# A message-passing kernel: the first edge layer and the middle node stage in one block

## The reference

```
h = maximum(layernorm(x), 0)
x = x + L0(h, edge_index, edge_weight, edge_weight_n2)   # signed cosine propagation
h = maximum(layernorm(x), 0)
x = x + L1(h, edge_index)                                # MLP messages, MLP update

L0: Wh = h @ W + b;  Wr, Wc = Wh[row], Wh[col]
    sim = dot(Wr, Wc) / max(|Wr| |Wc|, 1e-8)
    base = adj_v * softplus(deg_coeff[0] * deg_v + deg_coeff[1]) * (row != col)
    prop_pos = segment_sum(base * relu(sim) * Wc, row);  prop_neg likewise of -relu(-sim)
    result = scale * (coeff[0] * prop_pos + coeff[1] * prop_neg + coeff[2] * Wh)
L1: msgs = mlp(concat(x[dst], x[src]));  agg = segment_sum(msgs, dst)
    result = mlp(concat(x, agg))
```

## Time and profile before

| | us |
|---|---|
| median of 3 runs | 2410.95 |
| profiled execution, its own time | 2418.68 |
| its span, first to last instruction | 2416.6 |
| first edge layer, first SP issue to last scatter issue | 205.16 to 1508.13 |
| middle node stage, first SP load to last DVE instruction | 1518.05 to 1641.07 |
| second edge layer, first SP issue to last DVE instruction | 1646.96 to 2190.36 |
| node stage 2, first SP load | 2193.05 |

### The profile page before, as it was taken

How to read it: one execution, slowest core, us unless ns; L and a number is a source line. 1 busy time by engine, 2 the same in 40 slices (tenths; PEclk the granted TensorE clock), 3 DMA queues, 4 the chain that set the end, 5 groups by cost and what they waited for, 6 DMA issues and landing times. The chain is left out here.

```text
span 2416.6 us, 57279 instructions
## 1 busy us (share of the span) xinstructions
PE 1562.8 (65%) x16004; PEld 1340.6 (55%) x16004; DVE 1553.3 (64%) x5636; ACT 864.0 (36%) x3093; POOL 1695.9 (70%) x1413
## 2 busy tenths in 40 slices
PE   4886755455555555555555550005999999997998
PEld 2555645455554545545455550004999999994554
DVE  5995655555555454554545552794999999995554
ACT  3773322222222222222222221462333333334665
POOL 2775888888888888888888886746777777761322
PEclk9996555555555555555555555556999999999999
DMA  3775544444444444444444432565555454534664
GB/s 100 251 247 172 114 82 80 77 83 75 84 79 78 84 74 85 80 77 83 75 86 73 84 47 18 170 221 146 128 124 126 124 126 124 126 81 119 188 188 145
DMA packets 342563, 273.11 MB, mean 113 GB/s; under 512 B 144834, under 2 KB 273514, under 8 KB 342484
## 3 DMA queue, kind: packets, MB, share of 16 engines
q1 hardware_dynamic: 259028, 233.22, 33.2%
q0 software_dynamic: 81536, 38.61, 15.0%
q10 hardware_dynamic: 1920, 0.37, 0.1%
HBM read 206.69 MB, written 65.34 MB: 113 GB/s over the span
## 5 line engine op out<-in xcount | busy, mean ns | idle before, releaser
L1117 POOL DMA_INDIRECT x<-e_sums,e_to x392 | 623.4, 1590 | 126.4 <-issue 118.6
L1352 PE MATMUL bank<-e_parts,e_same 128*128 128x64 bf16 x2940 | 172.8, 240 | 586.7 <-DVE e_parts L1211 586.7
L1304 PE MATMUL bank<-e_window,e_onehot 128*128 128x64 f32 x2352 | 525.0, 422 | 16.8 <-DMA e_window<-wh 16.8
L1304 PEld LDWEIGHTS bank<-e_window,e_onehot 128*128 128x128 f32 x2352 | 511.7, 332 | 16.9 <-DVE e_onehot L1143 16.9
L1102 POOL DMA_INDIRECT e_ends<-wh,e_ids x392 | 425.2, 1085 | 132.8 <-issue 102.1
L1352 PEld LDWEIGHTS bank<-e_parts,e_same 128*128 128x128 bf16 x2940 | 159.4, 129 | 602.8 <-issue 602.8
L829 POOL DMA_INDIRECT e_near_source<-h,e_near_ids x392 | 394.8, 1007 | 129.8 <-issue 117.4
L1250 ACT ACTIVATE e_sq<-e_ends 128x64 f32<-128x64 f32 x784 | 188.6, 241 | 686.0 <-DMA e_ends<-wh,e_ids 685.9
L1175 DVE SCALAR_TENSOR_TENSOR e_prod<-e_ends 128x64 f32<-128x64 f32 x392 | 65.7, 223 | 370.8 <-DMA e_ends<-wh,e_ids 370.8
L939 PE MATMUL bank<-e_near_to_edge,e_near_window 128*64 128x128 f32 x2352 | 153.4, 281 | 171.2 <-DMA e_near_window<-h 171.2
L939 PEld LDWEIGHTS bank<-e_near_to_edge,e_near_window 128*64 128x64 f32 x2352 | 130.0, 139 | 177.6 <-DVE e_near_to_edge L850 171.6
(11 more groups left out here) (150 smaller groups left out, 2860.9 us busy)
## 6 DMA issues: line engine op xcount, KB each, us to landing
e_window<-wh SPq DMA_DIRECT2D x392, 96.0 KB
e_near_window<-h SPq DMA_DIRECT2D x392, 96.0 KB
e_owners<-ends SPq DMA_DIRECT2D x98, 256.0 KB, 2.9
n_x<-x SPq DMA_DIRECT2D x98, 256.0 KB, 3.0
n_x<-in_x_dram SPq DMA_DIRECT2D x49, 256.0 KB, 2.8
wh<-n_wh SPq DMA_DIRECT2D x49, 256.0 KB, 2.0
x<-n_x SPq DMA_DIRECT2D x49, 256.0 KB, 2.3
e_rel<-rel SPq DMA_DIRECT2D x98, 128.0 KB, 3.2
```

The costliest lines, as they stand in the source:

```text
L1117: pool.indirect_dma_start(out=added_tab, out_offset=bass.IndirectOffsetOnAxis(ap=t.to[s][:, j:j + 1], axis=0), in_=t.sums[s][:, j, :], in_ ...
L1304: last = nc.tensor.matmul(bank[s % 2][:, j * D:(j + 1) * D], onehot, window, start=w == 0, stop=w == WK - 1)
L1352: last = nc.tensor.matmul(bank[6 + s % 2][:, i * D:(i + 1) * D], t.same[s][:, same_block(j, i), :], t.parts[s][:, part, j, :], start=j == ...
```

## The change

The block of the first edge layer and that of the middle node stage become one. The edge buffers are allocated and given back before the block, then `agg_sb` and the node stage's buffers are allocated, on the same addresses as before. In the one block each engine runs its edge program and then, with no barrier between, its node program. SP clears the first set of semaphores where it did, and then waits itself for the four `added` semaphores before it loads `x1`. The helper functions that were local to `edge_programs` become functions of the module (`both_ways`, `edge_sync`, `edge_gpsimd`, `edge_vectors`, `edge_scalars`, `edge_tensors`), with what they do unchanged.

```diff
@@ build
-        edge_phase(nc, c, tabs, layer=0, done=first)
-        first.give_back()
+        with ExitStack() as own:
+            edges = EdgeBuffers(c, Slots(nc, c, own, "e0"), 0)
         c["agg"] = sb("agg_sb", [P, NB * D])
         c["sems"] = Semaphores(nc)
-        node_phase1(nc, c, tabs, done=second)
+        edge_and_node_phase(nc, c, tabs, edges, first, second)
+        first.give_back()
         c["sems"] = Semaphores(nc)
-        edge_phase(nc, c, tabs, layer=1)
+        edge_phase(nc, c, tabs)
@@
-def node_phase1(nc, c, tabs, done):
+def edge_and_node_phase(nc, c, tabs, edges, before, done):
@@ block.sync
         def _(sp):
+            edge_sync(nc, sp, c, tabs, edges, edges, 0)
+            before.clear(sp)
+            for s in range(ESLOTS):
+                sp.wait_ge(edges.added[s], 16 * G * -(-(GROUPS - s) // ESLOTS))
+
             def store(s, k):
@@ block.vector
         def _(dve):
+            edge_vectors(nc, dve, c, edges, edges, 0)
+
@@ block.gpsimd
         def _(pool):
+            edge_gpsimd(nc, pool, c, tabs, edges, edges, 0)
+
@@ block.scalar
         def _(act):
+            edge_scalars(nc, act, c, edges, edges, 0)
+
@@ new
+        @block.tensor
+        def _(pe):
+            edge_tensors(nc, pe, c, edges, edges, 0)
+
```

More of the change, by code:

```diff
@@ L718, in _, with edge_phase @@
                                    (-3, normed)])
-def edge_phase(nc, c, tabs, layer, done=None):
+        @block.tensor
+        def _(pe):
+            edge_tensors(nc, pe, c, edges, edges, 0)
+def edge_phase(nc, c, tabs):
     with ExitStack() as ctx:
[L723 to L729, removed]
-        with nc.Block() as block:
-            edge_programs(nc, block, c, tabs, near, far, layer, done)
@@ L734, in edge_programs @@
[L734 to L776, removed]
@@ new lines, in edge_phase, with _ @@
+        with ExitStack() as own:
+            near = NearBuffers(c, Slots(nc, c, own, "e1"))
+        far = EdgeBuffers(c, Slots(nc, c, ctx, "e1"), 1)
+        with nc.Block() as block:
+            @block.sync
+            def _(sp):
+                edge_sync(nc, sp, c, tabs, near, far, 1)
+            @block.gpsimd
+            def _(pool):
+                edge_gpsimd(nc, pool, c, tabs, near, far, 1)
+            @block.vector
+            def _(dve):
+                edge_vectors(nc, dve, c, near, far, 1)
+            @block.scalar
+            def _(act):
+                edge_scalars(nc, act, c, near, far, 1)
+            @block.tensor
+            def _(pe):
+                edge_tensors(nc, pe, c, near, far, 1)
@@ new lines, in both_ways, with edge_sync, apart @@
+def both_ways(c, eng, close, apart):
+    is_near = eng.value_load(c["near"][0:1, 0:1], min_val=0, max_val=1)
+    with eng.If(is_near > 0):
+        close()
+    with eng.Else():
+        apart()
+def edge_sync(nc, sp, c, tabs, near, far, layer):
+    def apart():
+        edge_loads(nc, sp, c, tabs, far, layer, False)
+        if layer == 1:
+            for s in range(ESLOTS):
+                sp.wait_ge(far.added[s], 16 * G * -(-(GROUPS - s) // ESLOTS))
+            sp.dma_start(c["agg"][:].rearrange("p (b d) -> p b d", d=D),
+                         tabs["agg"][0:NB * P, :].rearrange("(b p) d -> p b d", p=P)).then_inc(far.numbers_in[0], 16)
+            sp.wait_ge(far.numbers_in[0], 16 * (1 + -(-GROUPS // ESLOTS)))
+    both_ways(c, sp, lambda: edge_loads(nc, sp, c, tabs, near, layer, True) if layer == 0 else near_sync(nc, sp, c, tabs, near),
+              apart)
@@ new lines, in edge_gpsimd, with edge_vectors @@
+def edge_gpsimd(nc, pool, c, tabs, near, far, layer):
+    both_ways(c, pool, lambda: edge_pool(nc, pool, c, tabs, near, layer, True) if layer == 0 else near_pool(nc, pool, c, tabs, near),
+              lambda: edge_pool(nc, pool, c, tabs, far, layer, False))
+def edge_vectors(nc, dve, c, near, far, layer):
+    both_ways(c, dve, lambda: edge_vector(nc, dve, c, near, layer, True) if layer == 0 else near_vector(nc, dve, c, near),
+              lambda: edge_vector(nc, dve, c, far, layer, False))
@@ L779, with edge_scalars, edge_tensors @@
+def edge_scalars(nc, act, c, near, far, layer):
+    both_ways(c, act, lambda: edge_scalar(nc, act, c, near, layer, True) if layer == 0 else near_scalar(nc, act, c, near),
+              lambda: edge_scalar(nc, act, c, far, layer, False))
+def edge_tensors(nc, pe, c, near, far, layer):
+    both_ways(c, pe, lambda: edge_tensor(nc, pe, c, near, layer, True) if layer == 0 else near_tensor(nc, pe, c, near),
+              lambda: edge_tensor(nc, pe, c, far, layer, False))
 class NearBuffers:
```

## The result

The changed kernel takes 2406.82 us (median of 18 runs) against 2415.58 us of the kernel before on the same chips (18 runs); ratio 0.9965, 95% interval 0.9955 to 0.9976. That is 0.35% less, where 0.31% was forecast. The forecast of 2403.4 us was made from three runs of before whose median, 2410.95, lies low among the eighteen (2408.41 to 2421.45), so the ratio is the better measure of the change. Taken by itself, 2406.82 us lies nearer to the first rival's 2406.2 than to the forecast; the profile has to decide between the two.

A forecast was written before the change was run, and what follows sets the result against it. The prediction saw POOL's scatters bounding before the seam, DVE behind it, and an all-idle hole between. Loads 7.65 us earlier less 0.15 for POOL gave 7.5 us, from 2410.95 to 2403.4 us; range 2402.3 to 2407.5.

The forecast's parts named there:

- the first rival: Middle seam: POOL's own passage remains the gate and the handshake is cheap; gain 4.5 to 5.5 us, time 2406.2; chance 0.17.
- What bounds it and the stock: Seam from first edge layer to middle node stage: all engines idle, 7.7 us to take; DVE's stage behind moves whole.
- The barrier goes: At the seam SP waits only for the scatters' landing; first load at 1510.4, gain there at most 8.4 us.
- The loads meet no other traffic: First `x1` loads start 7.65 us earlier, at 1510.4 instead of 1518.05, with no other traffic that they did not meet before.
- POOL: After its landing wait POOL jumps to the node code, ready at 1514.1 where 1513.95 is needed; 0.15 us charged.
- The number: Sum at the seam: 7.65 - 0.15 = 7.5 us gain, median 2410.95 to 2403.4 us, 0.31% less.
- the 1.4 us that the prediction took for a barrier: Seam from node stage 0 to first edge layer: last store's landing at 203.76 to SP's first DMA at 205.16.
- The 3.6 us that the prediction left unexplained: Rest of the hole after second code packet and 1.4 us of barrier, from 1514.4; perhaps collecting of reports behind scatters.
- The second rival: Middle seam: SP's node code isn't at hand when its wait ends; first load at 1515.1, gain 2.9, time 2408.0; chance 0.06.
- The third: Second edge layer's loop: shifted code crosses a page, each of 20 rounds fetches again, 68 us, time 2471; slower, chance 0.03.

The follow-up runs named there:

- told before the jump: Changed kernel, but SP waits for a semaphore POOL raises behind its own landing wait, before its jump; last scatter's issue end to first `x1` load 1.78 us.
- told after: Changed kernel, but SP waits for a semaphore POOL raises as its first node-stage instruction, behind its jump; last scatter's issue end to first load 4.25 us.
- drained and told: Changed kernel, but SP waits for a semaphore raised by a POOL drain behind its jump; scatter's issue end to first load 9.72 us; timed later, 2415.34 us, ratio 1.0002.

## Why the prediction was right

*What bounds it and the stock.* Right: the hole was on every path, and the node stage moved as a whole: from DVE's first total to its last instruction 120.45 us became 120.38.

*The barrier goes.* The load was put 2.27 us behind the scatter's issue (1510.4) and comes after 1.52. The landing was read from POOL's next scatter, and, as the bound allowed, at least 0.6 us of that was POOL's own way from wait to issue. Gain at the load 8.40 us, the upper bound, not 7.65.

*The loads meet no other traffic.* Wrong by 0.73 us: this step took the load's 2.57 us over unchanged. They came to 3.30, because POOL's jump now falls into the same moment and its code packet (at 1504.3 us in the profile after, 0.9 behind the load's issue) is in the load's way. With the packet out of the way, by code left out or by POOL's wait moved, it is 2.65 and 2.64 again.

*POOL.* Charged 0.15 us, measured nothing. The lateness was bounded by DVE's passage at the last seam, which holds a barrier; POOL's own jump is 2.47 us.

*The number.* The prediction put the gain at the first load 0.75 us too low, overlooked a loss of 0.73 on the load's way to DVE, and charged 0.15 for POOL that did not come: 7.5 + 0.75 - 0.73 + 0.15 = 7.67. The mechanism was right, but that the sum comes this close is luck: two errors of the same size with opposite signs.

*The first rival* was half right: the meeting of five engines is cheap (0.2 to 0.3 us) and the hole was POOL's passage. But that passage did not stay in the load's way. Of the 1.4 us that the prediction took for a barrier at the seam from node stage 0, 0.9 were not the barrier's: without the far way the same seam takes 2.80 us from the last store's issue, not 3.70. The 9.92 us are

| | us | from |
|---|---|---|
| last scatter's landing seen by SP | 1.5 | the changed kernel |
| handover from POOL | 0.3 | told before the jump, less the changed kernel |
| jump with its fetch | 2.5 | told after less told before |
| first drain after indirect DMAs | 5.5 | drained and told, less told after |
| the barrier over that handover | 0.2 | the kernel before, less drained and told |

The change takes POOL's jump and its drain off the path. By the reading above it does not take the drain out of the program, since the block still ends in a barrier, now behind the node stage. There it costs nothing that shows. POOL's last centring ends at 1623.52, SP issues stores until 1629.43, and SP begins the second edge layer 5.88 us after DVE's end, against 5.89 before the change. The 3.6 us that the prediction left unexplained, and laid to the collecting of reports, fall in the 5.5 us of the drain.

The Trainium skill ("Runtime: NRT & Kernel Launch", The launch sequence) puts the meeting of the five engines in the runtime's own barrier at about 355 ns. The 0.34 us of one more barrier agree. The Trainium skill also says (same page, Instruction fetch mechanics) that a taken branch to a page that isn't held forces a fetch before execution goes on. The one packet in the 2.47 us of the jump agrees.

*The second rival* fails: SP was ready. *The third* too: from 1790 to 2120 us in the profile after, the second edge layer's loop, only the data queues move.

```profile
q1 hardware_dynamic: 45290, 33.00, 35.9%
q0 software_dynamic: 8044, 8.26, 14.9%
```

## What to carry to other kernels

Where the last engine to arrive at a barrier is the one that has issued indirect DMAs, look for its drain, 5.5 us here, and not at the meeting, 0.2 to 0.3 us. Let another engine wait for the landing and put the stages in one block, or at least let the issuing engine go to the barrier without waiting while another waits (4.2 of the 8.4 us for an edit of three lines). Put POOL's wait for its scatters behind its jump, not in front, so that its code comes while the last ones are issued; here that gave 0.6 us more. At the one seam tried where the last engine is one that computes, no gain was seen: what was saved in front was paid again within three tiles.

## What was not expected of the hardware

The first drain on POOL after indirect DMAs takes 5.47 us, 4.41 with 13.6 us of compute in between, and two further ones 0.22 together; a block's end with no indirect DMA before it, with its drain and the barrier, fits in 3.20. A code packet of 8 KB that begins 0.9 to 1.6 us after the issue of a load of 256 KB comes with a landing 0.1 to 0.8 us later (2.83 to 3.36 us against 2.52 to 2.74). With no wait in front of the jump, both packets for the code behind it move before the issue of the last scatter begins (1496.0 to 1499.0 us against 1499.54).
